# Early-fusion block on Trainium2: row maxima with the causal mask on VectorE, steps written out, another beginning

## The reference

```python
h = patches(x) @ W_embed + b_embed + pos_embed      # 196 patches of 768 values -> 256
h = concat([h, txt], axis=1)                        # 64 x 228 x 256
# attention: 16 heads of 16, causal
q, k, v = heads(layernorm(h) @ {Wq, Wk, Wv}.T)
scores = where(causal, -inf, q k^T / 4); probs = softmax(scores)
h = h + (probs v) @ Wo.T + bo
# feed-forward, weights made ternary: sign(w) where |w| > 0.5 * mean(|w|), else 0
x = layernorm(h); u = gelu(rms_normed(x) @ up.T)
h = h + rms_normed(u) @ down.T
```

## Time and profile before

| what | value |
|---|---|
| median of three runs | 2130.81 us |
| the profiled execution | 2129.19 us, its span 2127.5 us |
| busy over the span: PE, PE weight load | 1987.2 us (93%), 1555.6 us (73%) |
| busy over the span: DVE, ACT, POOL | 1518.1 us (71%), 1295.5 us (61%), 882.0 us (41%) |
| two reductions of a unit, 256 times | 161.8 and 281.3 us |
| mask matmuls, 1024 | 154.7 us (busy time, overlaps between neighbours counted once) |
| instruction queues | 3.16 and 0.68 MB for 58231 instructions |
| loads at the start | 768, three of 1024, 228 and two of 114 KB; pixels of one pair 1176 KB |

### The profile page before, as it was taken

One profiled execution on the slowest core, in us unless ns is written; L12 is line 12 of the kernel. 1 busy time (PEld: TensorE's weight loads), 2 busy tenths in 40 slices (PEclk: granted clock), 3 DMA queues, 4 the chain that ended last, 5 costly groups with the idle time before them and its releaser, 6 DMA issues.

```text
span 2127.5 us, 58231 instructions
## 1 busy us (share of the span) xinstructions
PE 1987.2 (93%) x22914; PEld 1555.6 (73%) x22914; DVE 1518.1 (71%) x2838; ACT 1295.5 (61%) x2050; POOL 882.0 (41%) x1066
## 2 busy tenths in 40 slices
PE   2789999999999999999999999999999999999875
PEld 2567777777778777777777777877777777777654
DVE  4457778777777677777777767777677787777753
ACT  2346666666666566665666666666566666666552
POOL 0124444444444444443444433444444444444443
PEclk9899999999999999999999999999999999999988
DMA  3111111111111101111101111110111111110000
GB/s 129 25 41 41 48 52 48 32 44 40 52 48 52 47 25 42 49 47 53 48 27 49 41 50 49 50 46 27 43 49 48 52 48 33 43 43 25 28 27 23
DMA packets 62845, 93.74 MB, mean 44 GB/s; under 512 B 9619, under 2 KB 59255, under 8 KB 59497
## 3 DMA queue, kind: packets, MB, share of 16 engines
q1 hardware_dynamic: 62568, 89.90, 15.2%
HBM read 45.03 MB, written 14.94 MB: 28 GB/s over the span
## 4 chain that ended last, share of the span: by engine, by line
PE 85%; DVE 7%; issue 3%; ACT 2%; POOL 1%; DMA 1%; SPq 0%; POOLq 0%; DVEq 0%; ACTq 0%
PE dense L324 45%; PE score L324 25%; PE pvps L324 8%; PE dense L345 3%; PE dense L382 2%; DVE h L1010 1%; PE dense L371 1%; DVE mx L934 1%; POOL acc L1150 1%; DVE km L970 1%; DVE rs L894 1%; DMA borow<-bo 1%; ACT pr L664 1%; DVE st L922 0%; PE dense L533 0%
## 5 line engine op out<-in xcount | busy, mean ns | idle before, releaser
L1131 POOL TENSOR_SCALAR_AFFINE_SELECT pr<-pr 114x456 f32<-114x456 f32 x512 | 303.7, 617 | 939.6 <-ACT pr L664 939.5
L664 ACT ACTIVATE pr<-score 114x1368 f32<-114x1368 f32 x256 | 335.5, 1311 | 337.0 <-PE score L324 336.6
L933 DVE TENSOR_REDUCE mx<-score 114x4 f32<-114x456 f32 x256 | 161.8, 632 | 245.5 <-PE score L324 242.0
L934 DVE TENSOR_REDUCE mx<-score 114x4 f32<-114x912 f32 x256 | 281.3, 1099 | 0.0
L324 PE MATMUL score<-km,qs 32*114 32x114 f32 (+1 forms) x4096 | 222.0, 331 | 24.3 <-issue 16.0
L324 PE MATMUL dense<-wdn,g 128*114 128x256 bf16 x1024 | 239.2, 279 | 4.5 <-issue 4.0
L1150 POOL TENSOR_TENSOR acc<-acc,sq 128x456 f32<-128x456 f32 x192 | 234.0, 1219 | 12.6
L324 PE MATMUL dense<-wdn,gl 128*114 128x256 bf16 x1024 | 234.1, 274 | 0.0
L324 PE MATMUL pvps<-pr,vp 114*32 114x228 f32 (+1 forms) x4096 | 205.2, 318 | 0.5 <-ACT raw L736 0.5
L894 DVE RECIPROCAL rs<-rs 128x228 f32<-128x228 f32 x128 | 201.0, 1570 | 0.0
L324 PE MATMUL score<-qs,km 32*114 32x228 f32 (+1 forms) x4096 | 194.2, 306 | 0.0
(11 more groups left out here) (126 smaller groups left out, 4503.6 us busy)
## 6 DMA issues: line engine op xcount, KB each, us to landing
pix<-x SPq DMA_DIRECT2D x32, 1176.0 KB
rs<-raw SPq DMA_DIRECT2D x256, 57.0 KB, 2.0
cx<-raw SPq DMA_DIRECT2D x256, 57.0 KB, 2.0
out<-h SPq DMA_DIRECT2D x64, 228.0 KB
h<-txt SPq DMA_DIRECT2D x32, 64.0 KB, 7.9
g<-wqkvo SPq DMA_DIRECT2D x1, 1024.0 KB
h<-w_upT SPq DMA_DIRECT2D x1, 1024.0 KB
h<-w_downT SPq DMA_DIRECT2D x1, 1024.0 KB
```

The source lines that it names most:

```text
L664: act(pr[q % 2][:], score[0:R, :, 0:SW], ACT.Exp, scale=float(HD) ** -0.5).then_inc(a["exp"], 1)
L933: nc.vector.tensor_reduce(mx[:, b, 0, :, r], score[0:R, :, 0:R], AX.X, ALU.max)
L934: nc.vector.tensor_reduce(mx[:, b, 1, :, r], score[0:R, :, R:SW], AX.X, ALU.max).then_inc(v["max"], 1)
L1131: nc.gpsimd.affine_select(out=blocks, in_=blocks, compare_op=ALU.is_ge, fill=0.0, base=0, pattern=[[0, 4], [1, R]], channel_multiplier=-1) ...
```

## The change

It has three parts. First, `scores_rows` no longer issues the four mask matmuls, and `maxima_unit` has eight `tensor_tensor_reduce` in place of two reductions: each adds the mask to one block of one head in place (in PSUM) and gives the maximum of each row to one element of `mx`. The mask tile has the width of the scores, with zeros where nothing is masked. Second, `steps` writes out all 35 steps. Third, the beginning: the pixels of pair 0 are loaded first, the weights go to tiles of their own (`km`, `h`, `sq`, `gl`) under four semaphores, and the preparation is spread over step 0. DVE does the constants in unit 2, the low parts of the projection weights and the absolute sums in unit 3 and the ternary weights in unit 5 of step 0; PE's matmul over the sums is at the end of unit 3.

```diff
         def steps(body, eng):
-            for t in range(4):
-                body(t, t % 4)
-            with eng.Fori(4, NPAIR - 4, 4) as i:
-                for j in range(4):
-                    body(i + j, j)
-            for t in range(NPAIR - 4, NPAIR + 3):
+            for t in range(NPAIR + 3):
                 body(t, t % 4)
...
             load_pixels(0)
+            sp.dma_start(stage_e, w_embed).then_inc(s_we, 16)
+            sp.dma_start(posb[:], pos).then_inc(s_row, 16)
+            sp.dma_start(brow, b_embed).then_inc(s_row, 16)
+            sp.dma_start(borow[:], bo).then_inc(s_row, 16)
+            sp.dma_start(stage_a, wqkvo).then_inc(s_wa, 16)
+            sp.dma_start(stage_u, w_upT).then_inc(s_wt, 16)
+            for i in range(2):
+                sp.dma_start(stage_d[i], w_downT[:, 1024 * i:1024 * i + 1024]).then_inc(s_wt, 16)
...
-                    if isinstance(t, int) and t < 4:
-                        sp.wait_ge(v["w"], 11)
+                    if isinstance(t, int) and t == 2:
+                        sp.wait_ge(v["tern"], 3)
                         apart(sp)
...
                 for qb in range(2):
                     for i in range(4):
-                        mm(score[0:R, i, qb * R:qb * S + R], qs[...], km[...], start=True, stop=False, ...)
-                for i in range(4):
-                    o = score[0:R, i, 0:SW].rearrange("p (x w) -> p x w", w=R)[:, 0:3:2]
-                    last = mm(o, identb[0:R, 0:R], cmask[0:R]..., start=False, stop=True, ...)
+                        last = mm(score[0:R, i, qb * R:qb * S + R], qs[...], km[...], start=True, stop=True, ...)
                 last.then_inc(pe["s"], 1)
...
+                    if isinstance(t, int) and t == 0 and k == 3:
+                        eng.wait_ge(v["tsum"], 3)
+                        mm(score[:, 0, 0:3], onesf, tern[:, 0:3], start=True, stop=True).then_inc(pe["init"], 1)
...
             reorder(0, 0)
+            eng.wait_ge(s_we, 16)
+            act(we[0][:].rearrange("p a b -> p (a b)"), stage_e, ACT.Copy).then_inc(a["w"], 1)
             reorder(0, 1)
...
+            eng.wait_ge(a["w"], 1)
+            tt(we[1][:].rearrange("p a b -> p (a b)"), stage_e,
+               we[0][:].bitcast(F32).rearrange("p a b -> p (a b)"), ALU.subtract).then_inc(v["we"], 1)
...
-                nc.vector.tensor_reduce(mx[:, b, 0, :, r], score[0:R, :, 0:R], AX.X, ALU.max)
-                nc.vector.tensor_reduce(mx[:, b, 1, :, r], score[0:R, :, R:SW], AX.X,
-                                        ALU.max).then_inc(v["max"], 1)
+                for qb, w in enumerate((slice(0, R), slice(R, SW))):
+                    for i in range(4):
+                        s_ = score[0:R, i, w]
+                        last = nc.vector.tensor_tensor_reduce(
+                            out=s_, in0=s_, in1=cmask[:, w], scale=1.0, scalar=NEG, op0=ALU.add, op1=ALU.max,
+                            accum_out=mx[:, b, qb, i, r:r + 1])
+                last.then_inc(v["max"], 1)
...
+                    if isinstance(t, int) and t == 0 and k == 2:
+                        constants()
+                    if isinstance(t, int) and t == 0 and k == 3:
+                        weights_rest()
+                        absolute_sums()
+                    if isinstance(t, int) and t == 0 and k == 5:
+                        ternary()
```

More of the change, by code:

```diff
@@ L154, in build @@
         pvps = ctx.enter_context(nc.psum_tensor("pvps", [128, 512], F32))
-        s_w, s_pix, s_txt = sem("s_w"), sem("s_pix"), sem("s_txt")
+        s_we, s_wa, s_wt, s_row, s_pix, s_txt = [sem(f"s_{z}") for z in ("we", "wa", "wt", "row", "pix", "txt")]
         s_out = sem("s_out")
@@ L330, in three @@
                 return mm(ps, stat[1], mov[0], start=False, stop=stop)
[L333 to L336, removed]
+            eng.wait_ge(p["w"], 7)
             def pixels(pair, k):
@@ L349, in embed @@
             def embed(pair, m, ph):
+                if isinstance(pair, int) and pair == 0 and m == 0 and ph == 0:
+                    eng.wait_ge(v["we"], 1)
                 if ph == 0:
@@ L388, in queries_keys @@
                 ps = bank_of("qk", k)
+                if isinstance(pair, int) and pair == 0 and k == 0:
+                    eng.wait_ge(v["wa"], 1)
                 if k == 0:
@@ L422, in up @@
                 ps = bank_of("up", m)
+                if isinstance(pair, int) and pair == 0 and m == 0:
+                    eng.wait_ge(v["tern"], 3)
                 if m == 0:
@@ L751, in step @@
                 for k in range(8):
+                    if isinstance(t, int) and t == 0 and k == 2:
+                        eng.wait_ge(s_wa, 16)
+                        act(wa[0][:].rearrange("p a b c -> p (a b c)"), stage_a, ACT.Copy).then_inc(a["w"], 1)
                     if Cc and k == 1:
@@ L841, in _ @@
[L841 to L844, removed]
-            nc.vector.tensor_copy(sel[:], selv[:].rearrange("p (r o) -> p r o", o=1).broadcast_to([128, Q4, R]))
-            eng.wait_ge(s_w, 16 * 7)
-            nc.vector.tensor_reduce(tern[:, 0:1], hf, AX.X, ALU.add, apply_absolute_value=True).then_inc(v["w"], 1)
@@ new lines, in weights_rest, with absolute_sums @@
+            def weights_rest():
+                eng.wait_ge(a["w"], 2)
+                tt(wa[1][:].rearrange("p a b c -> p (a b c)"), stage_a,
+                   wa[0][:].bitcast(F32).rearrange("p a b c -> p (a b c)"), ALU.subtract).then_inc(v["wa"], 1)
+            def absolute_sums():
+                eng.wait_ge(s_wt, 16 * 3)
+                for i, src in enumerate((stage_u, stage_d[0], stage_d[1])):
+                    nc.vector.tensor_reduce(tern[:, i:i + 1], src, AX.X, ALU.add,
+                                            apply_absolute_value=True).then_inc(v["tsum"], 1)
@@ new lines, in ternary @@
+            def ternary():
+                eng.wait_ge(pe["init"], 1)
+                nc.vector.tensor_copy(tern[:, 0:3], score[:, 0, 0:3]).then_inc(v["tbound"], 1)
+                eng.wait_ge(v["tbound"], 1)
+                tt(tern[:, 1:2], tern[:, 1:2], tern[:, 2:3], ALU.add).then_inc(v["tbound"], 1)
+                eng.wait_ge(v["tbound"], 2)
+                ts(tern[:, 4:6], tern[:, 0:2], 0.5 / (D * FF), None, ALU.mult).then_inc(v["tbound"], 1)
+                ts(tern[:, 6:8], tern[:, 0:2], -0.5 / (D * FF), None, ALU.mult).then_inc(v["tbound"], 1)
+                eng.wait_ge(v["tbound"], 4)
+                up2, down2 = [z[:].rearrange("p a b -> p (a b)") for z in (wup, wdn)]
+                for i, (src, dst, w) in enumerate(((stage_u, up2, 0), (stage_d[0], down2[:, 0:1024], 1),
+                                                   (stage_d[1], down2[:, 1024:2048], 1))):
+                    ts(dst, src, tern[:, 6 + w:7 + w], None, ALU.is_lt).then_inc(v["tbelow"], 1)
+                    eng.wait_ge(v["tbelow"], i + 1)
+                    nc.vector.scalar_tensor_tensor(out=dst, in0=src, scalar=tern[:, 4 + w:5 + w], in1=dst,
+                                                   op0=ALU.is_gt, op1=ALU.subtract).then_inc(v["tern"], 1)
@@ L1119, in _ @@
                                         pattern=[[-1, 128]], channel_multiplier=1).then_inc(p["w"], 1)
-            nc.gpsimd.affine_select(out=cmask[:], in_=cmask[:], compare_op=ALU.is_ge, fill=NEG, base=0,
-                                    pattern=[[-1, R]], channel_multiplier=1).then_inc(p["w"], 1)
+            for i in range(2):
+                eng.wait_ge(p["w"], 5 + i)
+                rows = cmask[:, 2 * R * i:2 * R * i + R]
+                nc.gpsimd.affine_select(out=rows, in_=rows, compare_op=ALU.is_ge, fill=NEG, base=0,
+                                        pattern=[[-1, R]], channel_multiplier=1).then_inc(p["w"], 1)
             eng.wait_ge(v["w"], 1)
```

80 lines of the change are left out of this document (26 added, 54 removed).

## The result

The changed kernel takes 2147.65 us (median of 4 runs, 2145.26 to 2148.87) where the kernel before takes 2130.87 (2129.62 to 2132.44): ratio 1.0077, 95% interval 1.006 to 1.0094, so slower by 0.8%. The forecast was 2082. The profiled execution has a span of 2143.5 us, 16.0 more than before.

The account below looks back on a forecast made before the run. PE's queue was taken to bound the kernel, with DVE's round trip the limit at five of eight units. Maxima -7, writing out -23 and beginning -19 from 2129.2 gave 2080, so 2082 us as median; range 2025 to 2190.

Parts of the forecast that it names:

- What bounds the kernel, mask off PE: PE's queue sets the pace; dropping mask matmuls frees 0.43 us in each of 256 units, 110 us if nothing takes it back.
- D: Added DVE time of one unit's new maxima, fetches included: 0.75 us forecast, bounds 0.43, 0.67, 1.03 and 1.71.
- The slot table: Changes in the distances between column-score starts (C) of a pair's eight units, 0 to 7: sum -0.22 us a pair, -7 us.
- Unit 4: Distance C3 to C4: DVE's idle time shrinks, so it comes 0.05 us late; 3.42 for 3.61, -0.19 us.
- Unit 7: Distance C6 to C7, 8.30 us: a long fill of PE work, so the full -0.43 us is gained.
- Unit 1: Distance C0 to C1: DVE has no gap, maxima 6.53 us apart plus D; 7.28 for 7.06, +0.22 us.
- Writing out: All steps written out removes five loop branches of 4.5 us each: -23 us.
- The beginning: Short beginning: pixels at about 7 us, hidden rows at about 28 instead of 51.63; -19 us, bounds -12 and -26.
- The sum: Profiled execution 2129.2 - 7 - 23 - 19 = 2080, so 2082 us as median; the forecast itself had 38%.
- rival B: New maxima cost more, DVE's round trip replaces the mask; break-even D 0.97, fetch 0.068 us; 2145 us at 0.075; 28%.

Follow-up runs that it names:

- e5: Changed kernel with two plain reductions and no mask ahead of the maximum on either engine (still cleared behind the exponential): 2032.88 us, ratio 0.955 to before.
- e10: Changed kernel with the first four new instructions of a unit writing to a spare SBUF tile in bf16 instead of PSUM: 2109.32 us, ratio 0.9884 to before.
- e9: Changed kernel with four more new instructions a unit, writing to a spare tile without an accumulator fetch: 2291.28 us, ratio 1.0746 to before.
- e7: Changed kernel with POOL's sums of squares narrowed from 456 to 8 columns, leaving the feed-forward's norm incomplete: 2123.97 us, ratio 0.9973 to before.
- e3: Changed kernel with the old beginning, so new maxima and steps written out: 2155.15 us, ratio 1.0108 to before.
- e1: Kernel before with all steps written out and nothing else: 2108.44 us, ratio 0.9885 to before.
- e8: Changed kernel without mask ahead of the maximum, two plain reductions, and with DVE's step 0 queue reordered: 2021.78 us, ratio 0.9497 to before.
- e11: Changed kernel, new maxima kept, with DVE's step 0 queue reordered (position sum and ternary passes later): 2137.75 us, ratio 1.0032 to before.
- e6: Changed kernel with new instructions for the first half of the queries only, the second half one plain unmasked reduction: 2072.79 us, ratio 0.9737 to before.
- e4: Changed kernel with the old mask matmuls on PE and two reductions, so writing out and new beginning only: 2104.34 us, ratio 0.9871 to before.

## Why the forecast was wrong, step by step

**What bounds the kernel, mask off PE.** Right in the main: of the 0.43 us a unit e5, without mask and with the old reductions, gains 0.33 to 0.46 at units 2 to 6. It gains nothing at unit 7 and at unit 1.

**D.** Right in size, 0.74 for 0.75, and that by luck: the fetch and the fixed cost were taken 0.21 and 0.06 us a unit too high, and writing back to PSUM, 0.26, was left out. The fetch exists as a row of its own, as the Trainium skill has it in "VectorE: DVE Perf Modes", section "Two Vector instructions with no wait between them"; but it costs only 0.014 us and not 0.04 (0.197 with it in e10, 0.183 without in e9, both to SBUF), since the next main instruction starts with it. The main instruction has some 0.064 us of fixed cost (0.183 less 0.119 for its elements; 0.352 and 0.234 are 0.118 apart), where the forecast took 0.072 from the rows of before. The missing 0.037, in seven of the eight, comes with writing the result back to PSUM, which the forecast named as unmeasured and gave no bound of its own. That section's statement and the trace agree in the count of instructions. The section of the same page of the Trainium skill that the forecast also weighed, "The DRAIN you can't avoid", has the next operation wait for an empty pipeline, but adds that one which isn't held starts earlier. The trace is with the addition: the distances are below the rows' lengths throughout (0.352 us for rows of 0.43).

**The slot table.** This is the step that failed. That a unit costs what DVE's round trip leaves of PE's gain was right, and the sum was wrong: -0.22 us a pair forecast, +1.16 measured. Three of its eight entries failed.
Unit 4 (+0.50): "it comes 0.05 late". DVE's work of unit 3 was taken over with its old durations. They depend on when DVE and POOL meet: before, DVE's `gelu_lo` was slowed (1.01 us in the mean; 0.62 after), now its small operations are, and the whole stretch is longer by 0.37 us (7.94 for 7.57). e7 shows it by taking POOL's sums away; e10, where the moment shifts, agrees.
Unit 7 (+0.43): "long fills". PE had work enough, but that work itself waits for DVE's `aT_lo`, 0.61 us in each pair. The distance is 8.30 or 8.31 before, in the changed kernel, and in e5, e7 and e10, so it doesn't get shorter with the mask gone, for any D from 0 to 0.74.
Unit 1 (+0.37): DVE has no gap there, which the table had; PE's dense work in front of C1 also waits 0.75 us for `pT_lo`, which stands in DVE's queue behind the longer maxima of unit 0. And here too DVE meets POOL: ahead of `pT_lo` it copies four elements (`ve`), in 156 ns on the mean before and in 557 after. In this pair the copy starts at 1061.29 and ends at 1061.85; POOL's second clearing of what is above the diagonal ends at 1061.83. The maxima of units 0 and 1 are 7.57 us apart, 6.53 + 0.74 and 0.30 more. First DVE's row before, then DVE's and POOL's after:

```profile
L1036 DVE COPY ve<-mv 114x4 f32<-114x4 f32 x16 | 2.5, 156 | 0.0
```

```profile
L1054 DVE COPY ve<-mv 114x4 f32<-114x4 f32 x15 | 8.4, 557 | 0.0
```

```profile
1060.69 1.14 POOL L1152 TENSOR_SCALAR_AFFINE_SELECT pr<-pr 114x456 f32<-114x456 f32 x2 [5.49 <-ACT pr L661]
```

In e5 the copy takes 163 ns and 0 to 1 misses the table all the same, by the wait for `pT_lo`; so the miss has another make-up there. Neither the two waits nor this copy were removed alone, so what each is worth is read from the trace and not shown by a run.
In the first steps the forecast had nothing; e3 against e1 shows 8.9 us there. PE's waits for maxima add up to 22.9 us in the first 261 us, 12.3 before.

**Writing out.** Right: 22.6 us for 23, and no issue stall of a microsecond elsewhere in the steady part.

**The beginning.** Mis-sized: 4 to 8 us for 19. The pixels were there at 9.5 us for 7. DVE's first long operation, the low part of the embedding weights, stood behind a wait for the last of three row loads (15.86), and PE's small matmul then waited 5.1 us for the sums of absolute weights, so the hidden rows came at 36.8 for 28; and the bounds and ternary passes took 8.2 us for 6, in front of the bias:

```profile
15.86 0.69 DVE L835 TENSOR_TENSOR posb<-posb,xn 114x512 f32<-114x512 f32 x1 [14.71 <-DMA borow<-bo]
...
36.82 0.69 DVE L972 TENSOR_TENSOR h<-dense,posb 114x512 f32<-114x512 f32 x1 [1.62 <-PE dense L371]
...
48.65 0.15 DVE L986 SCALAR_TENSOR_TENSOR nb<-mv,rstd 114x4 f32<-114x4 f32 x1
```

PE then stood still for 13.3 us, and came back at a granted clock of 0.50 (51 to 59 us), the 1.2 GHz level: the same matmul is 0.58 us long there, and 0.37 at a granted clock of 1.00 (60 to 62 us).

```profile
50.96 1.78 PE L382 MATMUL dense<-ident,xn 114*128 114x114 f32 x8 [13.33 <-ACT xn L706]
...
54.66 0.58 PE L325 MATMUL dense<-aT_lo,wa_hi 128*128 128x456 f32 x1
...
59.72 0.37 PE L325 MATMUL dense<-aT_hi,wa_hi 128*128 128x456 f32 x1
```

e8 and e11 take the wait for the rows and the ternary passes out of the way and win 11.1 and 9.9 us. Of the 10.9 us by which e8's first score block is earlier than e5's, 9.5 are there at the bias (39.13 for 48.67), which is DVE's queue; the rest may be the clock, which from 50 to 60 us is 1.00 in e8 for 0.50 in e5. The hidden rows still come at 34.1 in e8, so some 6 us of the forecast's 28 stay missed.

**The sum.** Forecast -7 - 23 - 19 = -49; measured +43 - 23 - 4 = +16, with +16.8 between the medians, and rival B's price (2145 us, "DVE's round trip takes the place of the mask") was met by another way than its own: the fetch is far below its 0.068, and D is 0.74 and not 0.97. Of the 50 us between -7 and +43 some 44 are the three entries (1.38 a pair), and 7 to 9 the first steps. The chance of 28% for slower was too low for a time that moves by 20 us with each 0.1 us of D and by 32 with each microsecond of a pair. How the time follows D, all with the new beginning and written out, none with a mask on PE:

| | e5 | e6 | e10 | changed | e9 |
|---|---|---|---|---|---|
| D, us | 0 | 0.35 | 0.59 | 0.74 | 1.47 |
| us | 2032.9 | 2072.8 | 2109.3 | 2147.7 | 2291.3 |

With the mask on PE it is 2104.3 us (e4). So, by the line between e6 and e10, the mask on DVE would pay up to a D of some 0.55; no kernel here that adds the whole mask there gets below 0.59.

**The version that beats both** is e8: no mask ahead of the maximum on either engine, written out, beginning reordered, 2021.8 us, 5.0% under the kernel before. It rests on the softmax being free in what is subtracted, as long as a masked score isn't so much larger than all allowed ones that the exponentials vanish in fp32. That holds for the inputs here; for others it would have to be looked at.

## What to carry to other kernels

When an instruction moves from a full engine to a half-empty one, count the round trips that pass through it, not the busy share: here DVE at 74% could take 0.74 us more a unit only at the price of more than the 0.43 us saved. Where a unit's fill is itself fed by that engine, its saving is lost too, so each wait of the fill needs its own line in the table. And ask first whether the work must be done at all: the mask ahead of the maximum need not.

## What the runs showed of the hardware

- The fetch of DVE's accumulator has a row of 139 ns but takes 0.014 us of queue.
- Custom add-and-maximum on DVE: 0.183 us for 114 elements without fetch, 0.197 with it, 0.234 where it and the one before write back to PSUM.
- Operations of DVE with SBUF operands, even of 32 elements, end with POOL's two-input operation beside them: 1.09 us, where the same one took 0.19 in the kernel before. A copy of four elements lasts 0.56 us for 0.16 beside POOL's clearing of the probabilities. A difference of 0.15 us in D changed the time by 38 us, more than the table's 30, with fewer such meetings.
- A loop's branch cost 4.5 us for each four pairs (247 us); straight code of 55,684 (e1) and 57,222 instructions (the changed kernel) had no stall of over 0.4 us for "issue" from 261 to 1880 us.
